# Unit 0 moved up on TensorE and ScalarE, the turn of A split into halves, and GpSimd's clearing of T moved ahead

## The reference

```python
xn = _layernorm(x)
q, k, v = silu(causal_conv4(xn @ w))             # 16 heads, DK 16, DV 32
beta = sigmoid(xn @ b_w.T + b_bias + beta_bias) * 2
g = -exp(A_log) * softplus(xn @ a_w.T + dt_bias)
for each token t:                                # state S: (DK, DV) for each head
    S = S * exp(g_t)
    delta = (v_t - k_t @ S) * b_t
    S = S + outer(k_t, delta);  o_t = q_t @ S
attn = (o * rsqrt(mean(o*o) + eps) * silu(gate)) @ o_w.T
y = (silu(xn @ Wg.T) * (xn @ Wu.T)) @ Wd.T       # FP4 weights, group scales, hidden 1408
out = x + attn + y / sqrt(mean(y*y) + 1e-6)
```

## Time and profile before

| | |
|---|---|
| median of 3 runs | 3317.35 us (3311.32 to 3319.44) |
| the profiled execution's own time | 3330.78 us |
| its span, first to last instruction | 3328.9 us |
| TensorE busy | 3141.2 us (94%) |
| VectorE busy | 2488.1 us (75%) |
| GpSimd busy | 1909.2 us (57%) |
| ScalarE busy | 1665.0 us (50%) |
| mean granted TensorE clock | 0.982 of full speed |
| chain that ended last | TensorE 81%, VectorE 13%, issue 4% |

### The profile page before, as it was taken

How to read it: one execution, slowest core, us unless ns; L and a number is a source line. 1 busy time by engine, 2 the same in 40 slices (tenths; PEclk the granted TensorE clock), 3 DMA queues, 4 the chain that set the end, 5 groups by cost and what they waited for, 6 DMA issues and landing times.

```text
span 3328.9 us, 117697 instructions
## 1 busy us (share of the span) xinstructions
PE 3141.2 (94%) x45632; PEld 2256.7 (68%) x45632; DVE 2488.1 (75%) x5472; ACT 1665.0 (50%) x3306; POOL 1909.2 (57%) x2865
## 2 busy tenths in 40 slices
PE   5999999999999999999999999999999999999996
PEld 4676667666666766666767776666767667666664
DVE  6877777777777777777777777777777777777773
ACT  4544555444555445555445555445554455544452
POOL 4566555666555665555665556665556655566643
PEclk8999999999999999999999999999999999999997
DMA  3000000000000000000000000000000000000000
GB/s 118 8 21 21 5 18 21 20 21 15 9 21 21 21 21 5 18 21 20 21 15 12 18 21 20 21 14 10 21 21 20 21 5 18 21 20 21 15 3 21
DMA packets 34157, 64.93 MB, mean 20 GB/s; under 512 B 5216, under 2 KB 7008, under 8 KB 33632
## 3 DMA queue, kind: packets, MB, share of 16 engines
q1 hardware_dynamic: 29664, 52.12, 4.8%
q10 hardware_dynamic: 4096, 6.42, 0.5%
HBM read 41.75 MB, written 16.78 MB: 18 GB/s over the span
## 4 chain that ended last, share of the span: by engine, by line
PE 81%; DVE 13%; issue 4%; ACTq 1%; DVEq 0%; ACT 0%; POOL 0%; POOLq 0%
PE PS L1174 17%; PE PS L1130 13%; PE PS L1161 9%; PE PS L1162 9%; PE PS L1243 7%; PE PS L1383 7%; DVE arena L884 3%; PE PS L1229 3%; PE PS L1308 3%; DVE arena L971 2%; PE PS L1261 2%; PE PS L1279 2%; DVE arena L374 2%; PE PS L1398 2%; DVE arena L991 1%
## 5 line engine op out<-in xcount | busy, mean ns | idle before, releaser
L884 DVE SCALAR_TENSOR_TENSOR arena<-PS,sc,arena 128x256 f32<-128x256 f32 x2112 | 1005.7, 482 | 395.8 <-ACT arena L590 294.9
L1161 PE MATMUL PS<-xh,wgu 128*128 128x256 f32 x2816 | 865.9, 340 | 61.2 <-DVE arena L992 50.6
L590 ACT ACTIVATE arena<-PS,sc 128x256 f32<-128x256 f32 x704 | 332.4, 476 | 881.3 <-PE PS L1162 768.5
L1174 PE MATMUL PS<-wdn,inner 128*128 128x512 f32 x1408 | 677.9, 609 | 30.5 <-DVE inner L896 30.5
L1162 PE MATMUL PS<-xl,wgu 128*128 128x256 f32 x2816 | 698.6, 282 | 0.0
L1161 PEld LDWEIGHTS PS<-xh,wgu 128*128 128x128 f32 x2816 | 532.6, 189 | 171.0 <-issue 82.4
L492 POOL TENSOR_TENSOR arena<-arena,work 128x31 f32<-128x31 f32 (+15 forms) x992 | 548.6, 553 | 77.8
L1162 PEld LDWEIGHTS PS<-xl,wgu 128*128 128x128 f32 x2816 | 531.8, 189 | 83.2 <-issue 83.2
L488 POOL TENSOR_TENSOR work<-arena 128x31 f32<-128x31 f32 (+15 forms) x992 | 518.8, 523 | 98.9 <-DVE arena L971 11.9
L1130 PE MATMUL PS<-xnT,wqkv 128*128 128x256 f32 x2048 | 483.1, 387 | 20.7 <-ACT inner L570 11.0
L1130 PEld LDWEIGHTS PS<-xnT,wqkv 128*128 128x128 f32 x2048 | 382.3, 192 | 87.4 <-issue 15.1
(11 more groups left out here) (150 smaller groups left out, 4600.4 us busy)
## 6 DMA issues: line engine op xcount, KB each, us to landing
xt<-in_x SPq DMA_DIRECT2D x64, 256.0 KB, 3.3
obuf<-in_x SPq DMA_DIRECT2D x64, 256.0 KB, 2.8
out<-obuf SPq DMA_DIRECT2D x64, 256.0 KB, 2.0
wqkv<-in_wqkv ACTq DMA_DIRECT2D x1, 2048.0 KB, 14.3
arena<-in_gup ACTq DMA_DIRECT2D x2, 704.0 KB, 6.4
arena<-in_dns SPq DMA_DIRECT2D x1, 1408.0 KB, 12.0
wg<-in_wg ACTq DMA_DIRECT2D x1, 1024.0 KB, 19.9
wo<-in_wo ACTq DMA_DIRECT2D x1, 1024.0 KB, 16.9
```

Of the source, the lines that this page charges most:

```text
L590: eng.activation(fa[:, u % 4, :], PS[:, bank(u, 0), 0:NB * P], ACT.Copy, scale=sc[:, u % 2, KB * m:KB * m + 1]).then_inc(fa_scaled.sem, 1)
L884: eng.scalar_tensor_tensor(out=fa[:, u % 4, :], in0=PS[:, bank(u, k // 2), k % 2 * NB * P:][:, 0:NB * P], scalar=sc[:, u % 2, KB * m + k:K ...
L1161: eng.matmul(o, w, xh[:, k, :], start=True, stop=False)
L1174: ins = eng.matmul(PS[:, b, :], inner[:, m, b * P:(b + 1) * P], wdn[:, m, :], start=(m == 0), stop=(m == FM - 1))
```

## The change

Four edits. On TensorE, unit 0 stands right behind the last `q_times_s` and ahead of `p_times_u(0)`, where it stood behind `p_times_u(1)`; units 1 and 2 each come one block of P times U earlier, so that the last block stands behind unit 2 where it stood behind unit 1. The gate's blocks (1, 2) and (1, 3) each come one place earlier between `k_times_u(3)` and `q_times_s(3)`. On ScalarE, unit 0 stands behind the gate's copies and ahead of `masked_keys(1)`. On VectorE, `turn_a` is split: the half of rows i = 0 to 15 stands behind unit 3 and `hidden(1)`, the other half behind unit 5 and `hidden(2)`; who used to wait for one signal waits for two. On GpSimd, the clearing of T's buffer moves out of `solve` to stand behind `keys_for_state`.

```diff
-        a_turned = signal("a_turned", 1)
+        a_turned = signal("a_turned", 2)
...
-        def solve(eng, n):
+        def clear_solution(eng, n):
 
             if not n.first:
                 hold(eng, *t_turned.at(n.before(), 1))
...
             eng.memset(arena[:, 1024:2048:CH + 1], 1.0).then_inc(lt_eye.sem, 1)
+
+        def solve(eng, n):
+
             hold(eng, *lt_eye.at(n, 2))
-            hold(eng, *a_turned.at(n, 1))
+            hold(eng, *a_turned.at(n, 2))
...
                 keys_for_state(eng, t, n)
+                clear_solution(eng, n)
...
             gate_copy(0)
             gate_copy(1)
+            unit(0)
             masked_keys(1)
 
 
             queries()
-            unit(0)
             unit(1)
...
-                    eng.wait_ge(*a_turned.at(t, 1))
+                    eng.wait_ge(*a_turned.at(t, 2))
...
-            def turn_a():
-                if not n:
-                    return
-                eng.wait_ge(*a_done.at(n, NB))
-                eng.wait_ge(*gram_out.at(n, NB))
-                eng.transpose(la,
-                              kbq[:, :, :].rearrange("p b (h i) -> p i (b h)", i=CH)).then_inc(a_turned.sem, 1)
+            def turn_a(half):
+                if half == 0:
+                    eng.wait_ge(*a_done.at(n, NB))
+                    eng.wait_ge(*gram_out.at(n, NB))
+                s = slice(half * CH // 2, (half + 1) * CH // 2)
+                eng.transpose(la[:, s, :],
+                              kbq[:, :, :].rearrange("p b (h i) -> p i (b h)", i=CH)[:, s, :]).then_inc(a_turned.sem, 1)
...
             gram_products(1)
-            turn_a()
             hidden(0)
             unit(3)
             hidden(1)
+            if n:
+                turn_a(0)
...
                 hidden(m)
+                if m == 2:
+                    turn_a(1)
...
             gate(1, 1)
+            gate(1, 2)
             k_times_u(3)
-            gate(1, 2)
+            gate(1, 3)
             q_times_s(3)
-            gate(1, 3)
-
-
+
+
+            unit(0)
             p_times_u(0)
             turn_kqn(1)
             turn_q()
             p_times_u(1)
-            unit(0)
+            unit(1)
             p_times_u(2)
-            unit(1)
+            unit(2)
             p_times_u(3)
-            unit(2)
             unit(3)
             gram(0)
             gram(1)
```

## The result

| | before | changed |
|---|---|---|
| median | 3317.99 us (3311.32 to 3319.44, 4 runs) | 3345.55 us (3340.89 to 3348.25, 4 runs) |
| the profiled execution | 3330.78 us | 3348.25 us |
| its span | 3328.9 us | 3346.4 us |

The ratio is 1.0077, with a 95% interval of 1.006 to 1.0094: slower by 27.6 us between the medians. I forecast 3347 us and a range of 3320 to 3374.

A forecast was written before the change was run, and what follows sets the result against it. TensorE, nearly always busy, was taken to bound the kernel, with two waits on one VectorE queue. 31 tiles at 0.9 us give 28, the clock 2: 30 us on the 3317.35 median, 3347 us, range 3320 to 3374.

The forecast's parts named there:

- P: Moment VectorE's last Gram product ends and frees unit 5 on TensorE; claimed 6.77 us behind the last P times U block.
- The last block of P times U comes 1.65 us later: On TensorE, the new order delays this block's end by 1.65 us, taken between 1.40 and 2.13.
- the lower bound of 1.40: Smallest delay of the last P times U block, in us, if "issue" idle time and one gate-block changeover vanish.
- The wait at unit 1: On TensorE, unit 1 newly waits 0.81 us for ScalarE's copies out of banks 6 and 7.
- The halves take 1.0 us and give 0.9 back at unit 7, and unit 8 keeps the rest: VectorE's half turns of A: TensorE ends unit 7 0.75 us late; unit 8's additions, with 0.78 slack, allow +0.97.
- A tile grows by 0.9 us: Net delay from unit 8 to the tile's end on TensorE: 0.9 us in each of 31 tiles, 28 us.
- The clock adds 2 us: TensorE's lower clock comes oftener but costs less each time: +2 us in all, between -9 and +17.
- The solution's later start is hidden: GpSimd's solution waits for A's second half and ends 1.7 us later, covered by 1.33 us idle before VectorE's output.
- Clearing early brings nothing: GpSimd's 0.95 us clearing moves to idle time, but the solution then waits for A's second half: no gain.
- the last state update is hidden: `k_times_u(3)` comes 0.9 us later; VectorE's update starts later but ends as before, costing nothing.
- The last block would stand 8.3 us, not 6.6, behind the end of Q times S: Expected profile sign on TensorE: last block of P times U 8.3 us behind Q times S, where 6.6 before.
- second rival: Whole kernel: last block only 1.4 us later or less, lower clock gone, giving 3327 or 3315 us; chance 0.13.

The follow-up runs named there:

- run 13: Not a run label: the words say that the kernel before "had run 13 us below its own profile"; no run has this number.
- e7_unit1_later: Changed kernel with units 1 and 2 each put back behind a later block of P times U, unit 0 still first: 3327.99 us, ratio 0.9984 to the kernel before.
- e3_clear: Kernel before with only the clearing of T's buffer moved ahead on GpSimd: 3332.94 us, ratio 1.0003.
- e2_order: Kernel before with only the new order on TensorE and ScalarE, A turned in one piece: 3383.9 us, ratio 1.0154.
- c1: Changed kernel timed once more, in one group on one chip: 3342.81 us against 3336.23 for the kernel before, ratio 1.0028.
- c2: Changed kernel with both halves of A turned behind the Gram products in the first tile, last group: 3341.8 us, ratio 1.0025 to the kernel before.
- e6: Changed kernel with both halves of A turned right behind the Gram products in the first tile: 3339.01 us, ratio 1.0032 to the kernel before.
- e1: Kernel before with only the turn of A split into two halves: 3300.42 us, ratio 0.9901.
- e8: Kernel before with the turn of A split, both halves right behind the Gram products in the first tile: 3295.4 us, ratio 0.9903.
- e9: Kernel before with A turned in one piece, but behind unit 3 and hidden block 1: 3314.33 us, ratio 0.9958.
- c3: Kernel before with only the turn of A split, repeated in the last group: 3305.52 us, ratio 0.9925.
- c4: Kernel before with the turn of A split, both halves behind the Gram products in the first tile, last group: 3304.69 us, ratio 0.9918.
- e4: Changed kernel with ScalarE scaling unit 2 ahead of the two copies of the attention output: 3325.91 us, ratio 0.9992 to the kernel before.

## Why the prediction came out as it did

The direction and the mechanism were right; four of its terms were not of their size, and some of the errors cancelled. The order alone is slower, the halves alone are faster, and moving unit 2 on ScalarE moves P: these three runs show the mechanism by parts.

- *The last block of P times U comes 1.65 us later.* It was 1.42 in the tile shown and 1.34 in the mean. All of the "issue" time in the blocks went, so it is the lower bound of 1.40, or just under it. The wait at unit 1 was given as 0.81 and is 0.83.
- *P is 6.77 us behind that block's end.* Unit 5 starts 6.82 behind it before and after, and the run with unit 2 ahead of the copies shows why.
- *The halves take 1.0 us and give 0.9 back at unit 7, and unit 8 keeps the rest.* 1.08 us measured, and 0.91 from P to the second down product (7.87 to 6.96). No wait is left at the down product. The halves alone are 0.56 us a tile, where the terms above, 0.78 of slack less 0.1, gave 0.68.
- *A tile grows by 0.9 us.* The step that was mis-sized: 0.64 us without the lower clock, mostly as the first term was 0.2 to 0.3 too large. With the clock's gain it was 0.35, a tile of 101.49 us and not 101.9.
- *The clock adds 2 us.* Wrong in sign. It fell oftener, as I said, 19 times for 13, but cost nothing, as TensorE waits for VectorE in units 6 to 8 anyway; with that the 8.8 us that it had cost before were gone (9.3 by the tile). The 0.45 that I took for each fall to 0.86 was read from one tile; the others lost from nothing to 0.7. I had named this reason and counted it for less than it was.
- *The solution's later start is hidden.* Right in the 31 tiles whose feed-forward takes 47 us: VectorE's wait ahead of the output went from 50.9 to 23.7 us and TensorE saw none of it. Wrong in the first, which lost 4.5 us in the profile, 3.0 of them by this. I had read the slack of one tile in the middle and not of the tile without a `t`.
- *Clearing early brings nothing; the last state update is hidden.* Right, the first by its own run.
- *The last block would stand 8.3 us, not 6.6, behind the end of Q times S.* I had misread my own rows: 6.62 us (1591.87 - 1585.25) is the way from the start of the first block to the end of the last, and from the end of Q times S at 1584.27 it is 7.60. After the change it is 8.15 from there. The sum does not use this figure.

In the profile these make 17.5 us, where I had 30. The tile's own numbers, the last block 1.4 us later and the lower clock's cost gone, are those of my second rival, "nothing measurable", to which I gave 0.13. Between the medians it was 27.6, since the kernel before had run 13 us below its own profile; in the last group it was 6.6. So that 3347 met 3345.55 so closely is largely luck. The traces show two losses of the kernel before that the changed one does not have, the cost of the lower clock and the "issue" waits, and the second differs between the groups as the medians do. What made 3318 us of the first timing is open, and so is what sets how often the clock falls.

## What to carry to other kernels

Follow a wait to what starts the queue behind it, through every engine's fixed order: here the wait of TensorE for VectorE began at a block of small matmuls, by way of two copies on ScalarE, and work put ahead of that block made the wait longer. Test the parts of a bundle alone: the halves were worth 1%, and the order took it away with more. Read the slack in the first tile too. Before you count on a removed wait, ask what else was using that time: here the "issue" waits took its place.

## What the runs showed of the hardware

Two blocks of 64 small matmuls side by side left TensorE standing for "issue" in the second, mostly 0.85 to 1.6 us and 37.6 us in all (e7_unit1_later). With a feed-forward unit ahead of the block it was 0.2 to 0.5 us in most tiles (before), and in the changed kernel, where a wait of 0.8 us for ScalarE stands ahead of the third block, none in tiles 1 to 30 (after).

A stream transpose of 128x512 took 1.08 us and of 128x1024 1.97.

TensorE fell to 1.2 GHz behind waits of 1.6 and 1.0 us in 13 tiles of 32 (before) and in 22 (e3_clear), and in all 32 behind waits of 2.2 and 0.9 us (e2_order). Behind the longer wait without the second it was 19 to 21 tiles at 2.1 to 2.2 us (after, c1, c2 and e6), 3 to 6 at 1.6 us (e1, e8, e9, c3 and c4), and none at 1.4 us (e4). A fall cost nothing in the changed kernel and 0 to 1.9 us in the kernel before.
